# FFN codes of a cross-attention layer: transposed by DMAs from ScalarE's queue instead of on TensorE

## The reference

```python
x = x + xattn(layernorm(x), ctx, ctx, Wq, Wk, Wv, Wo)   # 32 heads of 32, 8 key/value heads
x = x + ffn(layernorm(x))

def ffn(x):                                  # x as bf16, H = 1024, I = 512
    qg, sg = quant(x, inv_gate)              # quant: xs = x * inv; scale = max|xs| / 127 per row
    qu, su = quant(x, inv_up)                #        q = clip(round(xs / scale), -127, 127)
    g = (qg @ w_gate.T) * sg * s_wgate
    u = (qu @ w_up.T) * su * s_wup
    inter = clip(silu(g) * u, -10, 10).astype(bf16)
    qi, si = quant(inter, inv_inter)
    return (qi @ w_down.T) * si * s_wdown
```

## Time and profile before

| | |
|---|---|
| device time, median of 3 runs | 784.54 us (783.48 to 785.12) |
| profiled execution: first to last instruction | 782.1 us |
| its own device time | not given apart; the median lies 2.4 us above the span |
| PE busy, share, instructions | 694.3 us, 89%, 5072 |
| DVE | 570.1 us, 73%, 820 |
| ACT | 271.4 us, 35%, 417 |
| POOL | 216.2 us, 28%, 170 |
| DMA queues | SP's 62.42 MB, 25.9% of 16 engines' span; GpSimd's 8.39 MB, 2.8% |
| mean granted clock of TensorE | 0.959 |

### The profile page before, as it was taken

One profiled execution on the slowest core, in us unless ns is written; L12 is line 12 of the kernel. 1 busy time (PEld: TensorE's weight loads), 2 busy tenths in 40 slices (PEclk: granted clock), 3 DMA queues, 4 the chain that ended last, 5 costly groups with the idle time before them and its releaser, 6 DMA issues.

```text
span 782.1 us, 13916 instructions
## 1 busy us (share of the span) xinstructions
PE 694.3 (89%) x5072; PEld 426.2 (54%) x5072; DVE 570.1 (73%) x820; ACT 271.4 (35%) x417; POOL 216.2 (28%) x170
## 2 busy tenths in 40 slices
PE   3866889999999999999999999999999999758843
PEld 2753475457755675467655775557646764333321
DVE  4744564699758975898669975897679966886663
ACT  4542344143414343233315342333314340433230
POOL 3020100442142503242244204241234213232331
PEclk9995799999999999999999999999999999989985
DMA  7465468411232232222141223213232003112000
GB/s 295 145 219 180 128 194 258 115 35 52 88 100 70 52 109 78 88 57 79 47 121 50 60 85 100 67 51 108 70 95 54 31 20 112 46 52 78 1 27 27
DMA packets 36256, 71.24 MB, mean 91 GB/s; under 512 B 8816, under 2 KB 17008, under 8 KB 36208
## 3 DMA queue, kind: packets, MB, share of 16 engines
q1 hardware_dynamic: 33920, 62.42, 25.9%
q0 software_dynamic: 2304, 8.39, 2.8%
HBM read 44.43 MB, written 8.52 MB: 68 GB/s over the span
## 4 chain that ended last, share of the span: by engine, by line
PE 54%; DVE 16%; issue 13%; POOL 6%; SPq 4%; DMA 3%; ACT 3%; DVEq 0%; POOLq 0%; ACTq 0%
PE bank L459 20%; PE bank L531 13%; PE bank L567 4%; POOL xs L1462 3%; PE bank L421 3%; PE bank_s L478 3%; PE bank_o L508 2%; PE bank L589 2%; POOL rstd L1447 2%; DVE neg_max L1160 2%; PE bank_d L512 2%; DVE amax L1197 2%; PE bank_s L496 2%; SPq L317 2%; SPq L297 2%
## 5 line engine op out<-in xcount | busy, mean ns | idle before, releaser
L459 PE MATMUL bank<-act_t_hi,wq_hi 128*128 128x256 f16 x512 | 140.6, 275 | 2.5 <-DVE act_t_lo L1123 2.1
L459 PE MATMUL bank<-act_t_hi,wq_lo 128*128 128x256 f16 x512 | 140.4, 274 | 0.0
L459 PE MATMUL bank<-act_t_lo,wq_hi 128*128 128x256 f16 x512 | 140.3, 274 | 0.0
L1160 DVE TENSOR_REDUCE neg_max<-bank_s 128x4 f16<-128x512 f32 x128 | 82.4, 684 | 46.5 <-PE bank_s L478 46.3
L1169 DVE RECIPROCAL o_norm<-bank_d 128x512 f32<-128x512 f32 x32 | 107.3, 3353 | 12.2 <-PE bank_d L512 11.1
L1467 POOL TENSOR_TENSOR o_t_lo<-o_norm,o_t_hi 128x512 f16<-128x512 f32 x32 | 40.0, 1250 | 220.2 <-ACT o_t_hi L912 220.2
L898 ACT ACTIVATE probs<-bank_s 128x512 f32<-128x512 f32 x128 | 71.6, 596 | 78.6 <-PE bank_s L496 48.1
L531 PE MATMUL bank<-wo_hi,o_t_hi 128*128 128x512 f16 x256 | 97.4, 380 | 0.8 <-POOL o_t_lo L1467 0.8
L531 PE MATMUL bank<-wo_hi,o_t_lo 128*128 128x512 f16 x256 | 97.1, 379 | 0.0
L531 PE MATMUL bank<-wo_lo,o_t_hi 128*128 128x512 f16 x256 | 97.0, 379 | 0.0
L1462 POOL TENSOR_TENSOR xs<-xb,inv_up 128x1024 f32<-128x1024 bf16 x16 | 34.3, 2141 | 110.8 <-ACT code_g L947 110.8
(11 more groups left out here) (107 smaller groups left out, 1292.8 us busy)
## 6 DMA issues: line engine op xcount, KB each, us to landing
inp<-in_ctx_t SPq DMA_DIRECT2D x16, 512.0 KB, 4.8
inp<-in_x SPq DMA_DIRECT2D x16, 512.0 KB, 3.4
q_stack<-q_st_hi SPq DMA_DIRECT2D x128, 64.0 KB, 2.0
x<-in_x SPq DMA_DIRECT2D x16, 512.0 KB, 4.8
out<-x POOLq DMA_DIRECT2D x16, 512.0 KB, 3.0
q_stack<-q_st_lo SPq DMA_DIRECT2D x64, 64.0 KB, 2.0
x<-in_wo SPq DMA_DIRECT2D x6, 512.0 KB, 3.8
x<-in_wq SPq DMA_DIRECT2D x4, 512.0 KB, 6.5
```

Of the source, the lines that this page charges most:

```text
L459: ins = nc.tensor.matmul(bank[:, :, jj, :], wq_sb[a][:, 2 * item + jj, kc, :], act_t[m][:, kc, :, :], start=(kc == 0 and (a, m) == PARTS[0 ...
L1160: nc.vector.tensor_reduce(neg_max[:, c:c + REP], bank_s[g % 2][:, :].rearrange("p (j n) -> p j n", j=REP), AX_X, ALU.max, negate=True).the ...
```

## The change

`tq` and `ti` are gone from TensorE, and with them the names tg, tu and ti from the bank order and the semaphore `tq_full`. `qt` on ScalarE no longer copies a bank: it issues a DMA that transposes the codes from code_g, xb or inter straight into q_t, and raises `qt_ready` by 16 at its landing. All that waited for `tq_full` now waits for `qt_ready`. The places of `qt` in ScalarE's queue stay the same. `gu` waits for the banks' users in their new order.

```diff
 S3 = {n: i for i, n in enumerate(
     ["wo00", "wo01", "wo10", "wo11"] +
-    [f"{n}{b}" for b in range(2) for n in ("tg", "gate", "tu", "up", "ti", "dna", "dnb")])}
+    [f"{n}{b}" for b in range(2) for n in ("gate", "up", "dna", "dnb")])}
...
-            def tq(p, b, side):
...
-                for kc in range(KC):
-                    ins = nc.tensor.transpose(bank[:, kc * P:(kc + 1) * P], codes[u][:, kc * P:(kc + 1) * P], ident16[:, :])
-                ins.then_inc(tq_full, 1)
-
             def gu(p, b, name):
...
-                pe.wait_ge(qt_ready, 3 * r + u + 1)
-                if u == 1:
-                    pe.wait_ge(gu_scaled, 2 * r + 1)
-                elif b == 0:
-                    pe.wait_ge(resid, 4 * p + 4)
+                pe.wait_ge(qt_ready, 16 * (3 * r + u + 1))
+                if b == 0:
+                    pe.wait_ge(resid, 4 * p + 3 + u)
                 else:
-                    pe.wait_ge(dn_scaled, 4 * p + 2)
+                    pe.wait_ge(dn_scaled, 4 * p + 1 + u)
...
-            def ti(p, b):
...
             def dn(p, b, n):
...
-                pe.wait_ge(qt_ready, 3 * r + 3)
-                if n == 0:
-                    pe.wait_ge(gu_scaled, 2 * r + 2)
+                pe.wait_ge(qt_ready, 16 * (3 * r + 3))
+                pe.wait_ge(gu_scaled, 2 * r + 1 + n)
...
             def qt(p, b, u):
                 r = 2 * p + b
-                name = ("tg", "tu", "ti")[u]
                 n = (KC, KC, FC)[u]
-                bank = bank3[S3[f"{name}{b}"] % 2][:, :].bitcast(F16)
-                act.wait_ge(tq_full, 3 * r + u + 1)
+                src = (codes[0][:, :], codes[1][:, :], inter[:, :].bitcast(F16))[u]
+                if u < 2:
+                    act.wait_ge(code_ready, 2 * r + u + 1)
+                else:
+                    act.wait_ge(code_i_ready, r + 1)
                 if u == 0:
                     if needed(2 * r):
                         act.wait_ge(dn_full, 2 * r)
                 else:
-                    if needed(2 * r + u):
-                        act.wait_ge(gu_full, 2 * r + u)
-                nc.scalar.copy(q_t[:, 0:n, :].rearrange("p c n -> p (c n)"), bank[:, 0:n * P]).then_inc(qt_ready, 1)
+                    act.wait_ge(gu_full, 2 * r + u)
+                passed(act, p)
+                act.dma_start(q_t[:, 0:n, :], src, transpose=True).then_inc(qt_ready, 16)
...
             def code(p, b, u):
                 r = 2 * p + b
                 if u == 0 and needed(3 * r - 2):
-                    act.wait_ge(tq_full, 3 * r - 2)
+                    act.wait_ge(qt_ready, 16 * (3 * r - 2))
...
                 if needed(3 * r - 1):
-                    dve.wait_ge(tq_full, 3 * r - 1)
+                    dve.wait_ge(qt_ready, 16 * (3 * r - 1))
                 nc.vector.tensor_scalar(xb[:, :], x2[b][:, :], mv2[:, b, 0:1], rstd2[:, b:b + 1],
                                         ALU.subtract, ALU.mult).then_inc(xb_ready, 1)
...
                 if needed(3 * r):
-                    dve.wait_ge(tq_full, 3 * r)
+                    dve.wait_ge(qt_ready, 16 * 3 * r)
```

More of the change, by code:

```diff
@@ L181, in build @@
         code_ready = sem("code_ready")
-        tq_full = sem("tq_full")
         qt_ready = sem("qt_ready")
@@ L536, in wo_ @@
                     ins.then_inc(wo_full, 1)
-            def tq(p, b, side):
[L539 to L542, removed]
-                if u == 1:
-                    pe.wait_ge(qt_ready, 3 * r + 1)
-                elif b == 0:
-                    pe.wait_ge(resid, 4 * p + 3)
-                else:
-                    pe.wait_ge(dn_scaled, 4 * p + 1)
-                for kc in range(KC):
-                    ins = nc.tensor.transpose(bank[:, kc * P:(kc + 1) * P], codes[u][:, kc * P:(kc + 1) * P], ident16[:, :])
-                ins.then_inc(tq_full, 1)
             def gu(p, b, name):
@@ L704, in steady @@
                 wo_(prv, 1, 1, 7, 8)
-                tq(prv, 0, "g")
                 k(nxt, 0, 1)
@@ L709, in steady @@
                 gu(prv, 0, "gate")
-                tq(prv, 0, "u")
                 pv(cur, 0, 1)
@@ L715, in steady @@
                 xt(nxt, 0, 0)
-                ti(prv, 0)
                 xt(nxt, 0, 1)
@@ L723, in steady @@
                 dn(prv, 0, 1)
-                tq(prv, 1, "g")
                 s(cur, 1, 2)
@@ L739, in steady @@
                 gu(prv, 1, "gate")
-                tq(prv, 1, "u")
                 q(nxt, 1, 3)
@@ L755, in steady @@
                 q(nxt, 2, 3)
-                ti(prv, 1)
                 for n in range(0, 4):
@@ L794, in finish @@
                 st(last, 0, 1)
-                tq(last - 1, 0, "g")
                 for n in range(2, 6):
@@ L801, in finish @@
                 gu(last - 1, 0, "gate")
-                tq(last - 1, 0, "u")
                 gu(last - 1, 0, "up")
                 pv(last, 0, 1)
-                ti(last - 1, 0)
                 dn(last - 1, 0, 0)
                 dn(last - 1, 0, 1)
-                tq(last - 1, 1, "g")
                 s(last, 1, 0)
@@ L813, in finish @@
                 mt(last, 1)
-                tq(last - 1, 1, "u")
                 gu(last - 1, 1, "up")
@@ L818, in finish @@
                 pv(last, 1, 0)
-                ti(last - 1, 1)
                 st(last, 1, 6)
@@ L844, in finish @@
                 wo_(last, 1, 1, 7, 8)
-                tq(last, 0, "g")
                 gu(last, 0, "gate")
-                tq(last, 0, "u")
                 gu(last, 0, "up")
-                ti(last, 0)
                 dn(last, 0, 0)
                 dn(last, 0, 1)
-                tq(last, 1, "g")
                 gu(last, 1, "gate")
-                tq(last, 1, "u")
                 gu(last, 1, "up")
-                ti(last, 1)
                 dn(last, 1, 0)
```

## The result

The changed kernel takes 879.84 us (median of 4 runs, 875.9 to 884.35) against 784.01 for the kernel before: 12.1% slower, ratio 1.1208, 95% interval 1.1147 to 1.1269. The forecast was 838, in a range of 800 to 895: sign and range hold, the point is 42 us low. The profiled execution took 884.35 us, 1.65 more than its span. It is the longest of the four and 4.5 above the median, so differences read from its trace come out a few us larger than those of the medians.

What follows compares the result with a forecast made beforehand. TensorE's queue in its written order was taken to bound the kernel. Six passes adding 36.5 us and the finish 16.7 gave 53.2, on the median of 784.54 a forecast of about 838, range 800 to 895.

Steps and rivals of the forecast that it cites:

- L: Time from issue to landing of a large (256 KB) transposing DMA, taken as 3.5 us, bounds 2.4 and 4.9.
- M: Time from issue to landing of a small (128 KB) transposing DMA, taken as 2.8 us, bounds 2.0 and 3.7.
- 3 L + M - 7.2: Time added to each of the six passes, from the landing times: 6.1 us a pass, 36.5 in six.
- Steps 1 to 4: Gate, up, down of batch 0, then gate of batch 1 in a pass: nothing, 2.4, 1.7, 1.3 us; together 4.7.
- Step 5: Up of batch 1 in a pass, its DMA issued after the late gate: 2.05 us more, together 6.3.
- late and cold: Rival: up of batch 1 meets the next pass's loads (9 us in six passes), clock falls (12): 859; chance 0.08.
- step 3: Down of batch 0 in a pass, waiting for a small DMA: 1.7 us more, together 4.1; TensorE idles near 3.
- 12 in all: Cost over the six passes if TensorE's clock falls in them, 2 us a pass; no fall was taken.
- 7 L + 4 M: The landing times contained in the finish's loss, which was forecast at 16.7 us.
- ScalarE's held queue: Each DMA issue holds ScalarE's queue, 0.6 us if like SP's, for L at most; costed at nothing.
- Not slower: Rival: landing so quick that the cover holds, sign turning at 1.8 us; 775 at 1.4; chance 0.04.
- Block by block: Rival: the DMA works off 128-column blocks in turn, landing after 6.2 us large, 3.7 small: 925; chance 0.12.

Runs made afterwards that it cites:

- experiment 6: Kernel before, with only batch 1 of the six passes transposed by DMA, two q_t and gate's DMA issued early: 784.24 us against 786.18, ratio 0.9969.
- Experiments 2: Changed kernel with a second xb buffer, so ln2_apply of batch 1 waits for no DMA: 860.37 us, 1.0942 of the kernel before.
- experiment 5: Changed kernel with two q_t and up's codes written to u_buf instead of xb: 806.19 us, 1.0247 of the kernel before.
- experiment 1: Changed kernel with SP holding the next pass's loads until up's DMA of batch 1 has landed: 855.9 us, 1.0872 of the kernel before.
- experiment 4: Changed kernel with a second q_t buffer and gate's DMA of batch 1 issued before mt_copy; xb single: 829.36 us, 1.0531 of the kernel before.
- experiment 7: Changed kernel plus 30 unread products a pass, ahead of the waits before down of batch 0 and up of batch 1: 872.7 us, 1.1123 of before.
- experiment 9: Changed kernel with the last two pairs back on TensorE transposes and ScalarE copies: 858.88 us, 1.0942 of the kernel before.

## Why the prediction was right, and where its sizes were off

**Removal.** 1.13 us of TensorE a round: experiment 6 lost 1.3 us a pass for one round. Right.

**Landing.** L was taken at 3.5 and M at 2.8; the medians are 3.2 to 3.3 and 2.5. The bounds held for the medians, and not for up of batch 1: in five passes its DMA took 6.4 to 7.8 us, over the 4.9 of the bound and over the 5 that the prediction named as a sign of being wrong. With 3.2 and 2.5 the rule 3 L + M - 7.2 gives 4.9 us a pass, not 6.1. These two sizes alone would have made the forecast too high.

**Steps 1 to 4.** Right in place and near in size. Gate of batch 0 waits for nothing, with a landing of 3.6 to 3.9 us in a slack of 4.3. VectorE's xb waits 2.30 us (2.4 was said), `v` stands behind it, down of batch 0 idles 2.35, gate of batch 1 0.67. Experiments 2 and 5 took the xb wait away and got its time back.

**Step 5 failed.** "Gate is done at 369.06 + 4.7 = 373.8, and the DMA lands at 377.4" has L = 3.5 in it. The DMA took 7.8 us, since SP had just issued three loads of 512 KB. The rival "late and cold" had this place, and priced it at 5 us, 9 in all; it cost 24 to 27 (experiment 1). The 4.9 it used was the slowest copy of 128 KB. That copy (v_cur at 152.33) stood right behind a load of 512 KB (151.89), so it was already a DMA that met loads, with fewer ahead of it. The trace of before held a nearer row: of the three loads in a burst at 367.45, 368.17 and 368.87, the first landed after 3.4 us and the third after 5.8. The Trainium skill (DMA: Bandwidth & Descriptors, Queues, rings and completion order) says that every DMA engine takes turns between the queues that have work. This trace shows no such turns for the first 4.4 us: up to 408 us the loads' queue alone moved data. The load that was issued 0.4 us ahead took 7.3 us, the transposing DMA 7.8. Whether its packets had not reached the engines yet or stood in line there, no run here shows.

**The clock failed.** "In step 3 TensorE would idle near 3 us, less than in that row, so I take no fall." It idled 2.35 us, and the stretch from 385 to 391 stands at 0.73 of 2.4 GHz, so partly at 1.2; eight products after 6.24 us took 3.59 us. The rows of before already spoke against the argument: up at 702.05 took 3.26 us, though no wait in the 8 us before it was longer than its own 1.44. Of the 12.4 us a pass, 4.9 are the rule at measured landings and 4.5 the loads; the remaining 3.0 I put down to the clock. That is a remainder, not a measurement of its own. The sixth pass, which meets no loads, gives the same: 93.35 against 85.25 is 8.1, less 4.9 is 3.2. Beside it stand the 3.8 us by which TensorE's busy time in the third pass exceeds that of the same work at full clock (experiment 4), part of it hidden, and the 10.7 us that came back in six passes when the idle time was filled (experiment 7), against 6 x 3.0 = 18. The "12 in all" kept as a bound was of the right size, and wrongly left out of the sum.

**The finish.** 7 L + 4 M at measured landings is 13.4 us, 23.4 were lost. Up of batch 0, the first step, came 3.2 us late where 1.7 were forecast; its DMA took 4.1 us. Up of batch 1 came 10.1 late for 6.6, the first gate of the last pair 13.6 for 9.3, the last down 23.3 for 16.7. So the excess grew along the whole finish, from 1.5 to 6.6 us. TensorE idles there 59.8 us, before 40.2: 19.6 more. And it is busy 3.8 more although four rounds of transposes (4.5 us) are gone: 8.3 us of clock, which falls to 0.79 from 0.89. Not all of that is lost time, and some is chance: with the code of before (experiment 9) TensorE was busy 100.95 us at 0.85, 5.0 more than before, and the finish only 3.5 us longer. TensorE at three places of the tail; before, the same up took 1.90 at 743.84 and the same gate 1.90 at 757.78, while the last up was slow already, 3.05 at 762.28:

```profile
835.96 3.27 PE L549 MATMUL bank<-w_up,q_t 128*128 128x512 f16 x8 [3.89 <-DMA q_t<-xb]
...
854.24 3.60 PE L549 MATMUL bank<-w_gate,q_t 128*128 128x512 f16 x8 [3.25 <-DMA q_t<-code_g]
861.05 3.59 PE L549 MATMUL bank<-w_up,q_t 128*128 128x512 f16 x8 [3.22 <-DMA q_t<-xb]
```

Each of these waits for L is followed by products at little more than half the rate. How the slow products and the waits overlap was not taken apart further.

**The sum against the spans.** Forecast +53.2, measured +100.6: passes 38.0 more than forecast, finish 6.7, start 2.7. By the medians it is +95.8. The sign "A pass of 91 to 92 us although TensorE has lost over 20 us of busy time in all" did not come: a pass took 97.8, and TensorE was busy 16.5 us longer. That 879.84 still lay in the range is owed to a wide range, whose upper part stood for landings of 4.9 everywhere; the loss came by another way.

**What was costed at nothing.** ScalarE's held queue: 1.25 us a DMA, not 0.6, and it cost nothing that shows: every pass of experiment 6 has three such DMAs, and they average 85.0 us against 85.4. The last four passes of experiment 5 have six and take 85.4. Right.

**The rivals.** Not slower: out, no landing was under 2.4 us. Block by block: out, eight blocks land in 3.2 us and four in 2.5, so a block more costs 0.2 us at most. The page of the Trainium skill quoted for it (VectorE: DVE Perf Modes, The three transpose paths) gives 1309 ns for one block; the trace shows that this can't be multiplied. Late and cold: both of its mechanisms happened, with 24 to 27 us for its 9 and some 18, by the remainder, for its 12. It was given 0.08 as a case apart; it should have been part of the forecast.

## What to carry to other kernels

Moving work off the bounding engine by a DMA pays only where the landing is covered: put the 3 us, and what is in flight on all queues at that moment, against the slack of each place, and let every place without slack keep the old way. A DMA that reads and writes single buffers holds both ends until it lands, so look for who writes the source next. Here freeing both ends gave back 74 of the 96 us (experiment 5), in part because the DMA then went ahead of the loads. Idle time on TensorE of 2 to 3 us is to be priced once without and once with slow products behind it: after 2.3 us the same four products took 1.03 us in one kernel and 1.88 in another.

## What the runs showed of the hardware

A transposing DMA within SBUF lands 3.1 us after its issue at best for 128 x 1,024 16-bit values and 2.4 for 128 x 512, a plain copy 2.3 and 2.0. It holds the issuing queue for 1.25 us (median of 16), a plain one for 0.47. The Trainium skill (Advanced Engine Details and Errata, X-Bar Transpose (TRN2)) says that transposing DMAs are as fast as regular ones; for these sizes the trace shows 3.2 against 2.4.

Issued just behind three loads of 512 KB on another queue, a DMA of 256 KB lands after 6.4 to 7.8 us transposing and 6.1 to 7.1 plain (five passes each). The transposing one that took 7.8 us had no packet moved before 4.4 us, while the loads' queue moved 1.17 MB.

The changed kernel's four runs spread by 8 us (875.9 to 884.35), the longest at a mean granted clock of 0.907 and the shortest at 0.914. The kernel before spread by 2.4 us in the four runs beside it, but by 6.8, 9.2 and 10.5 in later sets of 7, 17 and 17 runs, so the wider spread is not shown to be the change's doing.
